# Attention stage reordered by batches of four heads: what runs between the score products

## The reference

```
x = x + 0.5 * ffn(layernorm(x))          # dense 256x256 + shared rank 16 + 6 routed experts of rank 16, top 2
x = x + attention(layernorm(x))
x = x + 0.5 * ffn(layernorm(x))

attention(x):
    k, q, v = x Wk', x Wq', x Wv'        # 16 heads of 16
    k = layernorm(k) * kln_g + kln_b     # q alike; both times 256 ** -0.25
    att = softmax(causal(q k'))          # 4096 x 4096 for each head
    return (att v) Wo' + bo
```

## Time and profile before

| | us |
|---|---|
| three runs | 1440.22, 1441.83, 1442.79 |
| median | 1441.83 |
| profiled execution, its own time | 1442.3 |
| profiled execution, span | 1440.6 |
| PE busy | 1234.8 |
| ACT busy | 1015.8 |
| DVE busy | 498.7 |

### The profile page before, as it was taken

How to read it: one execution, slowest core, us unless ns; L and a number is a source line. 1 busy time by engine, 2 the same in 40 slices (tenths; PEclk the granted TensorE clock), 3 DMA queues, 4 the chain that set the end, 5 groups by cost and what they waited for, 6 DMA issues and landing times.

```text
span 1440.6 us, 22376 instructions
## 1 busy us (share of the span) xinstructions
PE 1234.8 (86%) x8536; PEld 428.5 (30%) x8536; DVE 498.7 (35%) x1557; ACT 1015.8 (71%) x1102; POOL 204.4 (14%) x347
## 2 busy tenths in 40 slices
PE   0466787779988999999899998999999999999984
PEld 0342333323342334223332222322222322121233
DVE  2655555544725461435222343122123102020014
ACT  0112345455757787878878789798999999999950
POOL 1023322211111121111210111001001000000000
PEclk9777799799999999999999999999999999999985
DMA  4002200210020002000110000200000200000000
GB/s 105 17 8 67 69 7 1 69 36 1 9 78 20 1 16 74 16 1 1 45 59 1 1 2 9 70 13 1 1 1 15 69 7 1 1 1 1 8 8 15
DMA packets 39770, 33.36 MB, mean 23 GB/s; under 512 B 8883, under 2 KB 39594, under 8 KB 39658
## 3 DMA queue, kind: packets, MB, share of 16 engines
q1 hardware_dynamic: 37746, 31.74, 7.5%
q10 hardware_dynamic: 1912, 0.12, 0.1%
HBM read 18.72 MB, written 12.85 MB: 22 GB/s over the span
## 4 chain that ended last, share of the span: by engine, by line
PE 62%; ACT 13%; DVE 12%; issue 7%; SPq 3%; DMA 2%; POOL 1%; ACTq 0%; DVEq 0%; POOLq 0%
PE ps L958 57%; ACT ring L637 13%; PE ps L982 2%; DMA x<-in_x 1%; PE ps L1148 1%; SPq L522 1%; DVE oT L939 1%; PE ps L1042 1%; PE ps L1001 1%; SPq L506 1%; DVE st L668 1%; DVE xnT L691 1%; PE ps L1156 1%; DVE area L797 1%; DVE rstd L656 1%
## 5 line engine op out<-in xcount | busy, mean ns | idle before, releaser
L637 ACT ACTIVATE ring<-ps 128x1024 f32<-128x1024 f32 x1056 | 990.5, 1100 | 227.2 <-PE ps L958 224.9
L958 PE MATMUL ps<-ring,vf 128*17 128x512 f32 (+3 forms) x4608 | 568.8, 571 | 6.8 <-POOL ring L608 5.9
L958 PE MATMUL ps<-queries,keys 50*128 50x512 f16 (+3 forms) x2304 | 379.3, 371 | 34.0 <-DMA queries<-shift_d 9.2
L958 PEld LDWEIGHTS ps<-queries,keys 50*128 50x128 f16 x2304 | 93.5, 93 | 515.4 <-ACT ring L637 418.7
L608 POOL TENSOR_SCALAR_AFFINE_SELECT ring<-ring 128x256 f32<-128x256 f32 (+1 forms) x224 | 95.4, 444 | 555.5 <-ACT ring L637 552.0
L958 PEld LDWEIGHTS ps<-ring,vf 128*17 128x17 f32 x4608 | 80.5, 96 | 180.3 <-issue 152.3
L691 DVE COPY xnT<-ps 128x512 f32<-128x512 f32 x50 | 34.6, 691 | 155.4 <-PE ps L982 115.4
L764 DVE SCALAR_TENSOR_TENSOR x<-ps,x 128x512 f32<-128x512 f32 x32 | 22.1, 692 | 174.9 <-PE ps L958 174.8
L939 DVE COPY oT<-ps 128x512 f32<-128x512 f32 x32 | 22.1, 691 | 167.9 <-PE ps L958 167.8
L958 PE MATMUL ps<-baseT,xnT 128*128 128x256 f32 x256 | 75.9, 422 | 4.5 <-ACT area L631 2.0
L958 PE MATMUL ps<-qkT,xnT 128*128 128x512 f32 x128 | 68.1, 657 | 4.7 <-DVE att L946 1.9
(11 more groups left out here) (119 smaller groups left out, 788.6 us busy)
## 6 DMA issues: line engine op xcount, KB each, us to landing
parts_d<-split SPq DMA_DIRECT2D x32, 256.0 KB, 2.5
keys<-parts_d SPq DMA_DIRECT2D x96, 64.0 KB, 2.3
queries<-parts_d SPq DMA_DIRECT2D x192, 32.0 KB
x<-in_x SPq DMA_DIRECT2D x8, 512.0 KB, 5.0
out_x<-x SPq DMA_DIRECT2D x16, 256.0 KB, 2.2
queries<-shift_d SPq DMA_DIRECT2D x64, 4.0 KB
ring<-in_base_W SPq DMA_DIRECT2D x1, 256.0 KB, 4.6
ring<-in_Wq SPq DMA_DIRECT2D x1, 256.0 KB, 4.8
```

The costliest lines, as they stand in the source:

```text
L637: act.activation(probs[:, u % RING, :], bank(2 * (u % SLOTS), 2), ACTF.Exp, bias=0.0, scale=1.0).then_inc(exp_ok, 1)
L958: return pe.matmul(o, lhsT, rhs, start=start, stop=stop, skip_group_check=True)
```

## The change

The list goes batch by batch instead of unit by unit. For each batch come first the exponentials (and masks) of all its units, then the scores of the units up to three beyond its last, so usually of two units together; then a divide that is due, the values that are due, and then the side items of all units of the batch. Due times are counted in batches: values in their own batch's step, or in the next batch's step if they are masked. The divide comes in the step after the gather. The list of the first feed-forward is spread over one unit more. The steps themselves, their number and their waits on slots and ring are the same.

```diff
-            lists.append(spread(front(0, 0, c + 2), UNIT0[c], UNIT0[c + 1] - 2))
+            lists.append(spread(front(0, 0, c + 2), UNIT0[c], UNIT0[c + 1] - 1))
...
-    for u in range(NU):
-        yield "exp", u
-        if UNITS[u][3] is not None:
-            yield "mask", u
-        if u + 2 < NU:
-            yield from scores(u + 2)
+    ahead = 2
+    for b, (c, g, units, masked, first, last) in enumerate(BATCHES):
+        for u in units:
+            yield "exp", u
+            if masked:
+                yield "mask", u
+        for u in range(ahead, min(units[-1] + SLOTS + 1, NU)):
+            yield from scores(u)
             yield from fetch_ready()
-        b = BATCH_OF[u]
-        if BATCHES[b][2][-1] == u:
-            values.append((u + (2 if BATCHES[b][3] else 1), b))
-        if groups and groups[0][0] <= u:
+        ahead = max(ahead, min(units[-1] + SLOTS + 1, NU))
+        values.append((b + 1 if masked else b, b))
+        if groups and groups[0][0] <= b:
             yield "divide", groups.pop(0)[1]
-        while values and values[0][0] <= u:
-            b = values.pop(0)[1]
-            yield "values", b
-            if b in GROUP_END:
-                yield "gather", GROUP_END[b]
-                groups.append((u + 1, GROUP_END[b]))
-        for stage, n in side[u]:
-            yield stage, n
-            if stage == "heads" and n[1] >= 2:
-                split.add((n[0], n[1] - 2))
-                yield from fetch_ready()
+        while values and values[0][0] <= b:
+            v = values.pop(0)[1]
+            yield "values", v
+            if v in GROUP_END:
+                yield "gather", GROUP_END[v]
+                groups.append((b + 1, GROUP_END[v]))
+        for u in units:
+            for stage, n in side[u]:
+                yield stage, n
+                if stage == "heads" and n[1] >= 2:
+                    split.add((n[0], n[1] - 2))
+                    yield from fetch_ready()
```

## The result

The changed kernel took 1466.46 us at the median (1463.43 to 1467.54, 4 runs) against 1442.31 us (1440.22 to 1443.11) for the kernel before: 1.0166 times as long, 95% interval 1.0147 to 1.0186. It is slower by 24.2 us; forecast were 13.9.

A forecast was written before the change was run, and what follows sets the result against it. It took chunks 0 and 1 as bound by chains between engines, 2 to 5 mostly by PE, 6 and 7 mostly by ACT. Six terms summed to +13.9 us on the 1441.83 us median: 1456 us, range 1436 to 1474.

The forecast's parts named there:

- a: Merged scores: 84 more pairs of score units side by side on PE in chunks 1 to 5, 0.11 us saved each: -9.2 us.
- b: The divide at a group's end waits less for DVE's copy of the sums, 20 groups in chunks 1 to 5: -6 us.
- c: Values of a group's first masked batch come one unit later, holding up exp(5) and PE: +8 us.
- d: Long side items moved from between score units to behind values, chunks 5 to 7, 0.3 us each: +2.6 us.
- e: Side items run together wait for their one shared PSUM bank, 22 more such neighbours in chunks 1 to 5: +7.5 us.
- Term f: In chunks 0 and 1, ACT's copies of side items come behind two exponentials, 1.1 us more per affected batch: +11 us.
- The clock: Rival: longer idle PE in chunks 0 to 2 brings more time at 1.2 GHz, 20 us more, 1476 us; chance 0.12.
- The first rival: Gains from merged scores and the divide stand while the costs hide: 1430 us, spread 1430 to 1438; chance 0.18.

## Why the prediction held, and where it did not

The direction was right and the measured time lies in the range; the sum had +13.9, the runs +24.2. The places fit less well. Chunk 1 was to be 8 to 10 us longer and was 22.8. Chunks 3 to 5 were to stay within 3 us each; the terms come to about -2.5 for the three together (a -5.7, b -3.6, c +2.7, d +0.8, e +3.4), and they measured -9.2, with -5.7 in chunk 5. Chunks 6 and 7 were to be 2 to 3 us longer each and were 1.4 and 2.1. The two large misses have opposite signs, so that the total came out as near as it did is in part luck. The terms one by one:

- **Term f, the copies among the exponentials,** (+11) was right in its arithmetic: it had 2.4 us of idle PE in such a batch, and the rows show 1.60 + 0.53 = 2.1. Over chunks 0 and 1 the idle time that needs ACT as the reader is 12 us. Its naming of the cause, "exp, exp, copy", was half of it: ACT's order alone made the kernel faster by 0.64%. The cost comes from PE's order together with it. What f left out is the clock that comes with this idle time, another 10 to 13 us.
- **The clock** was a rival with 0.12 and not a term of the sum. By its own sign ("once PE's granted clock in chunk 1 falls from 0.91 to under 0.85") it holds: the clock fell to 0.80. It was priced at 20 us over chunks 0 to 2; PE's busy time there grew by 13.9. Rivals that come with the forecast's own mechanism don't exclude it: idle that I predicted should have been priced at the lower level as well. That 13.9 is near the 10 us that the sum lacks is partly chance, since other terms erred both ways.
- **Terms a and b, the merges and the divide,** (-9.2 and -6). In chunks 3 to 5 the two had 52 merges x 0.11 + 12 x 0.3 = 9.3, and the measured -9.2 is what they alone would give, as if c, d and e cost nothing there. No run separates a from these. Of b, moved alone in the old order, chunks 3 to 5 show 3.1 us where 12 x 0.3 = 3.6 was counted; it is mis-sized in chunks 0 to 2, where 9.8 us came and 2.4 were counted, chunk 0 at nothing. The row on the copy's wait held 18.8 us in all, and I took 6 from single groups. The weight loads of a pair were no obstacle to a: in chunk 4 of the change the pair at 613.70 is followed by values at 614.23, 0.53 us later as in the earlier trace rows.
- **Term c, the late masked values,** (+8). Taking them back won 12 us, but not by this mechanism alone: 4.5 in chunks 6 and 7 where 3.5 was summed, and 1.8 in chunks 3 to 5. The rest is in chunks 0 to 2, where PE's idle time did not change and its clock did. Its idle before exp(5) is as worked out (0.58 in the rows, 0.69 summed).
- **Term d, side items behind the values,** (+2.6) gave 0.9 in chunks 6 and 7 where 1.8 had been summed, and 0.9 again with the masked values early: twice too large. Its rows give 0.91 beyond the pace between score units, not "some 1.0".
- **Term e, bundles,** (+7.5). In chunk 1 without ACT's copies the new order has 4.8 us more idle PE, where 8 bundles were priced at 2.7; what part of it is c is not known. In chunks 3 to 5 its size stays open (3.5 us for bundles less merges in one pair of kernels, none that the medians can tell in the other).

The bounds of the six terms add up to 1416 to 1492, not 1421 to 1488; the range didn't rest on them.

The first rival (gains stand, costs hide) describes what chunks 3 to 5 do, and the variant confined to them; the early chunks outweigh it.

## What to carry to other kernels

When a list that orders several engines is regrouped, look for the pair of in-order queues that come to wait for each other: here PE's two score units behind its side items, and ACT's exponentials behind the copies of these items. Keep one piece of work that is free to run earlier between two side items, and let a short dependent step such as the divide come a unit late rather than stand at the head of others. Price idle time of PE in stretches that are already sparse with the lower clock that it brings, and apply a regrouping only in the stages whose bound it moves.

## What the runs showed of the hardware

I had not expected so much of the loss to be the clock. In chunk 1 of the change PE spent 55 of 138.5 us at 1.2 GHz, against 21 of 115.7 before; it was idle for half a us or more 26 times there, against 14. One projection takes 1.98 us at the one level and 3.78 at the other. And the level isn't fixed by the list: chunk 2 took 128.3 us in one execution and 135.3 in another, with the same 782 matmuls, 16.3 and 17.5 us of idle PE, and clocks of 0.97 and 0.92.
